# Four cross-attention layers on one core: a new static order of all engines, four group slots, and a residual transposed in 64-row tiles

## What is computed

```python
def L0(x, ctx):
    q, k, v = x @ Wq, ctx @ Wk, ctx @ Wv              # 16 heads of 64
    logits = einsum('bhqd,bhkd->bhqk', q, k) / 8 + col_bias
    out = einsum('bhqk,bhkd->bhqd', softmax(logits), v)
    return out @ Wo + bo + x
def L123(x, ctx):                                     # three times, own weights
    xn = x * rsqrt(mean(x * x) + eps) * norm_w
    q, k, v = xn @ wq, ctx @ wk, ctx @ wv             # 16 / 4 / 4 heads of 8
    p = softmax(einsum('btgrd,bsgd->bgrts', q, k) / sqrt(8))
    return x + einsum('bgrts,bsgd->btgrd', p, v) @ wo
```

## Time and profile before

| what | value |
|---|---|
| median of three runs | 1381.56 us (1379.52 to 1381.87) |
| profiled execution, first to last instruction (span) | 1376.3 us |
| median less span | 5.3 us |
| PE busy | 1362.7 us, 99% |
| DVE busy | 1064.6 us, 77% |
| ACT busy | 1003.3 us, 73% |
| POOL busy | 734.9 us, 53% |
| HBM | 16.42 MB read, 4.19 MB written |

### The profile page before, as it was taken

How to read it: one execution, slowest core, us unless ns; L and a number is a source line. 1 busy time by engine, 2 the same in 40 slices (tenths; PEclk the granted TensorE clock), 3 DMA queues, 4 the chain that set the end, 5 groups by cost and what they waited for, 6 DMA issues and landing times.

```text
span 1376.3 us, 59054 instructions
## 1 busy us (share of the span) xinstructions
PE 1362.7 (99%) x25494; PEld 1055.6 (77%) x25494; DVE 1064.6 (77%) x2258; ACT 1003.3 (73%) x2207; POOL 734.9 (53%) x851
## 2 busy tenths in 40 slices
PE   9999999999999999999999999999999999999997
PEld 7777777777777777777787777777777777777875
DVE  4487777987778977778777788777798777778776
ACT  4667777767778677777677786777776777767886
POOL 5355456654456545466554565544665445655553
PEclk9999999999999999999999999999999999999999
DMA  5010010000000010100001001001011010010000
GB/s 151 18 30 22 15 34 16 26 27 23 26 23 22 27 27 23 28 18 26 26 24 26 23 22 27 27 24 28 17 27 27 23 27 25 19 36 22 7 23 14
DMA packets 46003, 37.02 MB, mean 27 GB/s; under 512 B 17072, under 2 KB 41520, under 8 KB 45744
## 3 DMA queue, kind: packets, MB, share of 16 engines
q1 hardware_dynamic: 44576, 32.89, 8.8%
q10 hardware_dynamic: 1168, 0.36, 0.1%
HBM read 16.42 MB, written 4.19 MB: 15 GB/s over the span
## 4 chain that ended last, share of the span: by engine, by line
PE 95%; ACT 2%; DVE 2%; issue 0%; POOL 0%; DMA 0%; SPq 0%; POOLq 0%
PE psum L954 18%; PE psum L942 16%; PE psum L1009 10%; PE psum L1027 8%; PE psum L969 8%; PE psum L991 7%; PE psum L1055 7%; PE psum L1019 5%; PE psum L980 5%; PE psum L1063 4%; PE psum L1032 3%; PE psum L961 2%; PE psum L1038 2%; ACT E L1141 1%; ACT E L1136 1%; DVE st L1226 1%
## 5 line engine op out<-in xcount | busy, mean ns | idle before, releaser
L892 POOL TENSOR_TENSOR E<-E,st 128x512 f32<-128x512 f32 x488 | 497.3, 1044 | 168.1 <-DVE st L1238 159.4
L1136 ACT ACTIVATE E<-E,inv 128x512 f32<-128x512 f32 x384 | 273.4, 722 | 135.8 <-DVE E L1230 134.3
L1226 DVE TENSOR_REDUCE st<-psum 128x8 f32<-128x512 f32 x372 | 240.4, 673 | 145.5 <-PE psum L991 145.1
L1235 DVE TENSOR_REDUCE st<-E 128x8 f32<-128x512 f32 x488 | 321.2, 665 | 35.3 <-ACT E L1129 28.2
L1141 ACT COPY E<-psum 128x512 f32<-128x512 f32 x512 | 275.1, 609 | 33.7 <-PE psum L1009 33.5
L954 PE MATMUL psum<-wv,cT 128*128 128x374 f32 (+1 forms) x768 | 273.3, 486 | 0.3 <-issue 0.3
L1230 DVE TENSOR_TENSOR E<-psum,st 128x512 f32<-128x512 f32 x372 | 248.3, 677 | 0.3
L904 POOL TENSOR_TENSOR nt<-nt,powers 128x2 f32<-128x2 f32 (+1 forms) x102 | 19.9, 196 | 420.0 <-DVE nt L1265 400.2
L942 PE MATMUL psum<-cT,wk 128*128 128x256 f32 x1024 | 240.5, 383 | 0.2 <-DMA cT<-in_ctx_t 0.2
L942 PEld LDWEIGHTS psum<-cT,wk 128*128 128x128 f32 x1024 | 191.5, 190 | 34.8 <-issue 1.5
L954 PEld LDWEIGHTS psum<-wv,cT 128*128 128x128 f32 x768 | 138.2, 189 | 73.5 <-ACT V L1097 8.5
(11 more groups left out here) (68 smaller groups left out, 1632.2 us busy)
## 6 DMA issues: line engine op xcount, KB each, us to landing
KB<-K SPq DMA_DIRECT2D x1536, 8.0 KB
cT<-in_ctx_t SPq DMA_DIRECT2D x32, 256.0 KB, 2.8
xq<-in_x_t SPq DMA_DIRECT2D x32, 128.0 KB, 2.1
out<-xT SPq DMA_DIRECT2D x30, 128.0 KB, 1.8
wk<-in_L_xattn_Wk SPq DMA_DIRECT2D x3, 256.0 KB, 5.8
wv<-in_L_xattn_Wv SPq DMA_DIRECT2D x2, 374.0 KB, 8.6
wq<-in_L_xattn_Wq SPq DMA_DIRECT2D x1, 512.0 KB, 7.7
wo<-in_L_xattn_Wo SPq DMA_DIRECT2D x1, 512.0 KB, 4.4
```

The lines of the kernel that those rows point to most:

```text
L892: e.tensor_tensor(E3, E3, wide(stat[s][u][:, 16:24]), ALU.mult).then_inc(g_nrm.sem, 1)
L1136: e.activation(E[s][u][:, :], E[s][u][:, :], ACT.Exp, scale=inv[s][:, u // 2:u // 2 + 1]).then_inc(a_exp.sem, 1)
L1226: e.tensor_reduce(stat[s][u][:, 0:8].rearrange("p (r h) -> p r h", r=2), scores_of[g, l, u], AX, ALU.max).then_inc(d_max.sem, 1)
L1235: e.tensor_reduce(stat[s][u][:, 8:16], heads(E[s][u][:, :]), AX, ALU.add).then_inc(d_sum.sem, 1)
```

## The change

All tables are new (`PERIOD` from 42.042923 to 40.556641), and with them the order on PE, ACT, DVE, POOL and SP. `NS` goes from 3 to 4, so a fourth set of slot buffers exists. `t` is cut in two steps, one for each pair of units. The `x2` transpose is made of four transposes of 64 rows each, in the tile shape of `t`, into two neighbouring banks, and the `Square` on ACT reads both banks in one instruction. The number of all other instructions is as it was.

```diff
-NS = 3
+NS = 4
-PERIOD = 42.042923
+PERIOD = 40.556641
 PE_TIME = {
...
-    "t": {0: (-348.90236,), 1: (-317.45557,), 2: (-285.56016,), 3: (-253.49293,)},
+    "t": {0: (66.71164, 66.21564), 1: (98.14828, 97.59927), 2: (135.04492, 133.99991), 3: (176.09756, 175.10556)},
...
-                return [[("et", g, l, 2 * p + i)] for p in halves(g, u) for i in range(2)]
+                return [[("et", g, l, 2 * u + i)] for i in range(2)]
-            return [[st]] * (2 if kind == "pv0" else 1)
+            return [[st]] * (2 if kind in ("pv0", "x2") else 1)
...
+            elif st[0] == "x2":
+                at = min(([i, i + 1] for i in range(7)), key=lambda two: max(free[i] for i in two))
...
                 elif kind == "t":
                     w.wait_ge(l_ident, "ident")
-                    for n, p in enumerate(halves(g, u)):
-                        emptied(w, before[st][2 * n] + before[st][2 * n + 1])
...
-                            w.wait_ge(g_nrm, ("nrm", g, l, 2 * p), ("nrm", g, l, 2 * p + 1))
...
+                        w.wait_ge(g_nrm, ("nrm", g, l, 2 * u), ("nrm", g, l, 2 * u + 1))
+                    for r in range(2):
+                        for k in range(4):
+                            for i in range(2):
+                                rows, c = slice(64 * i, 64 * i + 64), 256 * r + 64 * k
+                                m = e.transpose(psum[:, at[i], c:c + 64],
+                                                E[s][2 * u + r][rows, 128 * k:128 * k + 128], ident[rows, rows])
+                    m.then_inc(p_t.sem, 1)
...
                     for p in halves(g, u):
-                        m = e.transpose(bank[:, 128 * p:128 * p + 128], xT[s][:, 128 * p:128 * p + 128], ident[:, :])
+                        for i in range(2):
+                            rows = slice(64 * i, 64 * i + 64)
+                            m = e.transpose(psum[:, at[i], 64 * p:64 * p + 64], xT[s][rows, 128 * p:128 * p + 128],
+                                            ident[rows, rows])
                     m.then_inc(p_ev.sem, 1)
...
+                    x = psum[:, at[0]:at[0] + 2, 64 * p[0]:64 * p[-1] + 64].rearrange("t i (p c) -> t i p c", c=64)
+                    sq = QT[s][:, 2, tokens].rearrange("t (p i c) -> t i p c", i=2, c=64)
...
-                        e.activation(QT[s][:, 2, tokens], bank[:, tokens], ACT.Square).then_inc(a_ev.sem, 1)
+                        e.activation(sq, x, ACT.Square).then_inc(a_ev.sem, 1)
```

More of the change, by code:

```diff
@@ L73 @@
+    "pv0": {0: (74.09363, 73.14963)},
+    "x2": {1: (85.65393,), 2: (107.24628,), 3: (147.52692,)},
+    "q": {1: (83.46957,), 2: (112.62527,), 3: (147.13092,)},
+    "pv": {1: (102.68927,), 2: (141.88290,), 3: (184.80255,)},
 }
 DVE_TIME = {
[L75 to L87, removed]
@@ L88 @@
[L88 to L93 removed]
+    "add": {0: (58.57864, 59.17365, 56.19662, 56.79163)},
+    "max": {0: (59.76865, 60.36465, 57.38663, 57.98264),
+            1: (86.44366, 85.41266, 88.45367, 89.04968),
+            2: (117.01025, 115.69727, 118.20227, 117.60626),
+            3: (150.75494, 149.56293, 150.15894, 151.94894)},
@@ L481 @@
+        "sum": {0: (62.86926, 63.80225, 61.45532, 62.05127)},
+        "rcp": {0: (63.57825, 64.51123, 62.64722, 62.76025)},
+        "wo0": {0: (81.60327, 81.86426)},
+        "sub": {1: (85.93298, None, 87.72290, None),
[5 rows of a table added]
     },
     31: {
-        "add": {0: (-119.87716, -119.6699, -122.49044, -123.16987)},
-        "max": {0: (-119.35079, -119.23138, -120.59121, -121.33631),
-                1: (-90.25966, -85.18078, -82.13575, -82.10246),
-                2: (-62.48423, -60.91201, -60.57903, -60.36904),
-                3: (-30.27588, -29.96241, -21.41472, -17.13109)},
@@ L498 @@
-        "sub": {1: (-90.24559, None, -81.0966), 2: (-61.3638, None, -60.0284), 3: (-29.3924, None, -16.06436)},
[3 rows of a table removed]
+        "add": {0: (53.34827, 53.94324, 50.96631, 51.56128)},
+        "max": {0: (54.53833, 55.13428, 52.15625, 52.75232),
+                1: (77.80493, 78.46899, 80.76501, 81.49402),
+                2: (96.34668, 95.75061, 96.94263, 97.53857),
+                3: (109.93762, 110.57263, 111.76660, 112.36267)},
+        "sum": {0: (59.50330, 60.32129, 57.74634, 58.34229)},
+        "rcp": {0: (60.21228, 61.24927, 60.09924, 59.18835)},
@@ L502 @@
+        "wo0": {0: (71.71191, 74.35901)},
+        "sub": {1: (79.06494, None, 82.08997, None),
[5 rows of a table added]
     },
@@ L627 @@
     [tuple(st) for _, *st in table] for table in (PE_TIMED, ACT_TIMED, DVE_TIMED, POOL_TIMED, SP_TIMED))
-DUE = {tuple(st): at for at, *st in ACT_TIMED + DVE_TIMED}
+TAKES = {"k": 0.59, "v": 0.48, "k3": 0.36, "q0": 0.6, "pv0": 1.09, "x2": 0.39, "q": 0.37, "pv": 0.36, "se": 0.6, "et": 0.61,
+         "exp": 0.72, "add": 0.68, "max": 0.68, "sub": 0.68, "sum": 0.67, "rcp": 0.19, "wo0": 0.47, "ssq": 0.41, "lr": 0.33,
+         "lm": 0.29, "wo": 0.42}
+DUE = {(kind, g, l, u): at + (1.1 if kind == "v" and u % 3 == 2 else TAKES[kind])
+       for at, kind, g, l, u in ACT_TIMED + DVE_TIMED}
 def halves(g, u):
@@ L795, in xattn_kernel @@
         p_s = signal("p_s", of(PE_ORDER, "s"))
-        p_t = signal("p_t", [("t", g, l, p) for _, g, l, u in of(PE_ORDER, "t") for p in halves(g, u)])
+        p_t = signal("p_t", of(PE_ORDER, "t"))
         a_ev = signal("a_ev", of(ACT_ORDER, *ON_ACT))
```

1030 lines of the change are left out of this document (605 added, 425 removed), and 76 rows, old and new, of tables (DVE_ENDS, PE_ENDS).

## The result

The changed kernel took **1456.16 us**, median of four runs (1451.34 to 1459.92), beside 1381.71 us for the kernel before in the same comparison: a ratio of 1.054, 95% interval 1.052 to 1.057. It is 75 us slower where 32 us less was forecast. The profiled execution has a span of 1452.9 us and a time of its own of 1454.71 us, so only 1.8 us lie around the span; the 5.3 us that the prediction added were for the most part the distance of one execution from the median.

A forecast was written before the change was run, and what follows sets the result against it. PE's own work was taken to bound the kernel: 1376.3 - 36.2 + 4 = 1344.1 us of span, plus 5.3 us gives 1349.4 us. Its own range was 1343 to 1355 us, widened to 1342 to 1363.

The forecast's parts named there:

- the 5.3 us that the prediction added: Whole kernel: added to the forecast span of 1344.1 us because the median lies that far above the span.
- What bounds the kernel: Whole kernel: PE, busy 1362.7 of 1376.3 us, sets the time; only 13.6 us are idle on it.
- Fewer stretches, and joins: PE's small-tile steps: 91 fewer entries save 18.2 us, joins inside stretches save 18.0 us, together 36.2 us.
- More wait instructions: PE's waits on POOL and banks, with t in two steps: some waits expected, 2 us in all in the middle.
- nothing for them: SP and its DMA queues: loads are issued tens of microseconds ahead, so no cost was counted.
- The bank burst (B): Banks at four t in a row: ACT one copy behind, 0.5 us wait a group, time 1363 us; chance 0.15.
- One price for every change of shape (A): PE, wherever one tile shape follows another: each change costs 0.16 us, time 1358 us; chance 0.12.
- POOL (C): POOL's layer 0 chain ends last: PE waits 2.4 us a group at t, time about 1421 us; chance 0.04.
- the dear `x2`: x2 as four 64-row transposes: each block costs what a whole 128x128 one does, up to 1377 us; chance 0.03.
- the lower bound: x2 in 64-row tiles: 0.125 us where t or x2 follows, as t is the same instruction on the same shape.
- The end: Last groups, with only their own chains: 2 us more idle time added to the 8.5 us in the last 76.
- 0.94 for faster: Whole kernel: chance of being faster by over 0.2%, all but C and half of the dear `x2`.

The follow-up runs named there:

- both orders wide: Changed kernel and kernel before, each with pv and layer 0's s and pv as half as many, twice-as-wide matmuls in groups 0 to 29: 1357.73 and 1370.01 us.
- the wide version: Changed kernel with pv and layer 0's s and pv as half as many matmuls of twice the columns in groups 0 to 29: 1357.73 us.
- the burst: Kernel before plus 1536 records of 64 columns at its start that compute nothing: 1427.59 us, one run.

## Why the prediction was wrong, point by point

- **What bounds the kernel.** Right that PE's work sets the time. Wrong by omission: PE also needs its instructions. The first section read "issue", 1.4 us, as a sign that nothing waits, and did not ask what "issue" was. It had the number that mattered within reach: 128 records of `pv` run in about 1.8 us (64 in 0.9), while 201 blocks in 1376 us are one per 6.8 us on average. On average the supply is ample; in a dense stretch it is not. What a block takes to arrive, though, the kernel before hardly shows: its only trace of it is 5 gaps.
- **Fewer stretches, and joins: -36.2 us.** The prices were nearly right. With the supply out of the way a middle group takes 40.57 us where 40.65 was forecast and 41.85 stood before. Like for like (both orders wide) it is 41.56 less 40.57, 0.99 us a group instead of 1.20; the wide steps save 0.29 us a group in the old order and about half of it in the new, which covers most of the difference. In the changed kernel itself the same gain is covered by 3.1 us a group of late instructions (43.65 us).
- **"More wait instructions", and "nothing for them": the step that failed.** The prediction went through PE's waits for banks, POOL and SP's queues, and put 2 + 2 us on them. For the middle that was about right: in the changed kernel PE's waits for ACT and POOL between 100 and 1300 us come to 3.0 us. The queue that it did not list, PE's own instruction queue, took about 90 us. The very thing that saves the changes of tile shape, small-tile steps side by side, takes away the long full-tile steps (8 records in 1.8 us) during which the next block arrives. Over the full-tile steps the supply has time to spare; over 416 records in 8.1 us (`t` takes about 34 ns a record, `s` of layer 0 16, `pv` 14) it has not.
- **The bank burst (B), 0.15.** Not what happened, though it was the closest in kind, a resource asked for faster than it is served. Halving the copies changed 1 us.
- **One price for every change of shape (A), 0.12.** Not borne out: between small shapes a change costs little at the entry. In the wide version a pair of `t` behind `s` of layer 0 takes 633.12 - 631.99 = 1.13 us, in the changed kernel behind `x2`, which has its own shape, 1.08: 0.05 us more, where A would show as 0.1.
- **POOL (C), 0.04, and the dear `x2`, 0.03.** C was the only case on the slower side; in the changed kernel PE never waited for POOL for more than 0.3 us at a time. `x2` cost close to what the lower bound said (0.30 us for two, 0.25 forecast).
- **The end, a second term that was too small.** 2 us were added. In the wide version PE is idle for 24.8 us in all, against the 13.6 + 4 that the sum allows, and 18.1 of them lie in the last 156 us, where the sum has 8.5 + 2 for the last 76. Even without the supply the forecast of 1344.1 us of span would have been 11.7 us too low, 7.2 of them idle time and 4.5 busy time (1331.0 against 1362.7 - 36.2).
- **The chances.** 0.94 for faster rested on a list of resources, each looked at and found sufficient. The list was not complete, and no chance was kept for that.

## What to carry to other kernels

Count the instructions of a dense stretch as you count its columns. Here PE was fed at 128 records per 3.5 to 4.3 us, about 31 ns each, and the first pause of the burst came after 223 records; a 64-column record in 128x32 tiles runs in 14 ns. By estimate from these, a stretch of more than some 200 such records needs longer ones between them. The stretch that paused had 416 records in 8.1 us, 19 ns each; with 256 in 8.24 us, 32 ns each, it ran through. Putting like with like saves 0.1 to 0.2 us per change of tile shape and cost 1.5 us per long pause here (89.3 us in 60); a kernel with few pauses of the kind "issue" may owe this to its mixed order.

In a profile, look for a pause inside one step, behind some of its records, with "issue" as its releaser, and compare its end with the transfers of the instruction queue. Short ones do not show as idle time: they make a step longer.

## What was not expected of the hardware

- The instruction queue of TensorE as a bound: 47.6 us for 1536 records of 64 columns, 42.4 us for 768 records of 256 columns with four times as many columns each.
- How abrupt it is: one `k` step of 1.8 us, moved by 3 us, is worth 34 us over 30 groups, 1.1 us a group.
- An edit that took 2880 records out of the kernel before made it 4 us slower, with 10.6 us of gaps behind instruction transfers instead of 4.3; taking out 6720 records made it 11 us faster.
- At the end of the wide version eight added matmuls lifted the granted clock from 0.50 to 1.00 and changed the time by nothing.
